# A two-layer cross-attention kernel on one core: last tile's end in two halves, weight loads on another queue, and a new written order

## What is computed

```
# layer 0
q = LN(x) @ Wq ; k, v = LN(ctx) @ Wkv                    # 16 heads
x = x + softmax(q k^T * hd**-0.5) v @ Wproj + bproj
x = x + gelu(LN(x) @ W1 + b1) @ W2 + b2                   # hidden 1024
# layer 1
q = unit(rotate(rms(x) @ wq)) ; k = unit(rotate(ctx @ wkv[k])) ; v = ctx @ wkv[v]
x = x + softmax(q k^T * hd**0.5) v @ wout
```

## Time and profile before

| what | us |
|---|---|
| median of 3 runs | 341.33 |
| lowest and highest | 341.09, 341.97 |
| the profiled execution's own time | 343.29 |
| span of its core, first to last instruction | 341.5 |
| TensorE busy (PE) in that span | 330.3 |
| VectorE, ScalarE, GpSimd busy | 266.7, 230.6, 193.2 |

### The profile page before, as it was taken

The page is one execution under the profiler, slowest core; times in us unless marked ns, Lnnn a source line. Parts: engine busy times, 40 slices in busy tenths (PEclk is TensorE's granted clock), DMA queues, the critical chain, the costliest instruction groups (busy, mean ns, idle before and its releaser), DMA issues.

```text
span 341.5 us, 10106 instructions
## 1 busy us (share of the span) xinstructions
PE 330.3 (97%) x3929; PEld 295.5 (87%) x3929; DVE 266.7 (78%) x586; ACT 230.6 (68%) x422; POOL 193.2 (57%) x200
## 2 busy tenths in 40 slices
PE   7899999999999999999999999999998999999995
PEld 7877876888778887899999999999998998888884
DVE  2969989988998669778788788666579989887643
ACT  3568876787775653885736665655678867789871
POOL 3585675886542202635857987493662799647100
PEclk9899999999999999999999999999999999999998
DMA  5667411110020000100000010000000000010101
GB/s 155 200 207 234 138 33 31 33 34 2 3 94 2 3 3 2 33 3 0 3 31 2 0 33 3 31 2 32 2 2 0 3 2 33 17 36 33 50 33 63
DMA packets 13007, 13.79 MB, mean 40 GB/s; under 512 B 1440, under 2 KB 12192, under 8 KB 12960
## 3 DMA queue, kind: packets, MB, share of 16 engines
q1 hardware_dynamic: 12240, 12.34, 11.4%
q10 hardware_dynamic: 720, 0.80, 0.8%
HBM read 11.04 MB, written 2.10 MB: 38 GB/s over the span
## 4 chain that ended last, share of the span: by engine, by line
PE 81%; DVE 6%; issue 4%; POOL 3%; ACT 2%; DMA 1%; ACTq 1%; POOLq 0%; DVEq 0%
PE banks_s L1326 12%; PE bank_y L1121 5%; PE banks_s L1216 5%; PE banks_s L1234 4%; PE banks_s L1393 4%; PE bank_o L1121 4%; PE bank_t L1337 4%; PE bank_y L1337 3%; PE bank_t L1121 3%; PE bank_o L1135 2%; PE bank_y L1135 2%; PE bank_o L1266 2%; PE bank_qk L1337 2%; PE bank_o L1337 2%; DVE row_max L2233 2%
## 5 line engine op out<-in xcount | busy, mean ns | idle before, releaser
L436 POOL TENSOR_TENSOR norm_q_inv<-norm_q_min,minus_half 128x32 f32<-128x32 f32 x8 | 43.8, 5476 | 21.0 <-DVE norm_q_min L2416 19.4
L424 POOL TENSOR_TENSOR norm_k_inv<-norm_k_min,minus_half 128x32 f32<-128x32 f32 x8 | 44.5, 5566 | 12.8 <-DVE norm_k_min L2383 12.7
L659 ACT ACTIVATE PT<-banks_s 128x1024 f32<-128x1024 f32 x32 | 31.0, 1023 | 15.7 <-PE banks_s L1243 15.7
L2233 DVE TENSOR_REDUCE row_max<-banks_s 128x8 f32<-128x1024 f32 x32 | 37.6, 1218 | 4.3 <-PE banks_s L1216 4.0
L703 ACT ACTIVATE W_s<-banks_s,small_t 128x256 f32<-128x256 f32 x60 | 25.2, 471 | 20.1 <-PE banks_s L1326 20.0
L1326 PE MATMUL banks_s<-lnT_hi,W_hi 128*128 128x256 f32 x120 | 34.4, 287 | 0.0
L1326 PE MATMUL banks_s<-lnT_hi,W_lo 128*128 128x256 f32 x120 | 33.9, 283 | 0.0
L1326 PE MATMUL banks_s<-lnT_lo,W_hi 128*128 128x256 f32 x120 | 33.9, 283 | 0.0
L685 ACT ACTIVATE PT<-banks_s 128x1024 f32<-128x1024 f32 x32 | 31.2, 1024 | 3.6 <-PE banks_s L1393 3.6
L712 ACT ACTIVATE hT_hi<-W_s 128x512 fp32r<-128x512 f32 x32 | 20.0, 632 | 15.8 <-PE bank_y L1337 10.1
L389 POOL TENSOR_TENSOR x_all<-x_all,b_row 128x256 f32<-128x256 f32 x16 | 12.4, 794 | 27.2 <-DVE b_xn L2316 25.4
(11 more groups left out here) (375 smaller groups left out, 1088.6 us busy)
## 6 DMA issues: line engine op xcount, KB each, us to landing
x_all<-in_x SPq DMA_DIRECT2D x16, 128.0 KB, 2.2
ctx_in<-in_ctx_wide SPq DMA_DIRECT2D x16, 128.0 KB, 2.5
W_s<-in_L_xattn_W SPq DMA_DIRECT2D x2, 1024.0 KB, 7.8
ctx_in<-in_ctx_T SPq DMA_DIRECT2D x8, 256.0 KB, 2.6
out<-x_all SPq DMA_DIRECT2D x16, 128.0 KB, 1.7
W_s<-in_L_xattn_Wq ACTq DMA_DIRECT2D x1, 256.0 KB, 3.4
W_s<-in_L_xattn_Wkv ACTq DMA_DIRECT2D x1, 256.0 KB, 4.5
W_s<-in_L_xattn_Wkv ACTq DMA_DIRECT2D x2, 128.0 KB, 4.8
```

The lines of the kernel that those rows point to most:

```text
L424: nc.gpsimd.tensor_tensor(norm_k_inv[:, :], norm_k_min[:, :], minus_half[:, :], ALU.pow).then_inc(c_kinv, 1)
L436: nc.gpsimd.tensor_tensor(norm_q_inv[:, :], norm_q_min[:, :], minus_half[:, :], ALU.pow).then_inc(c_qinv, 1)
L659: nc.scalar.activation(PT[:, t % 2, 2 * h:2 * h + 2, :], banks_s[:, 2 * h:2 * h + 2, :], ACT.Exp, scale=HD ** -0.5).then_inc(a_exped, 1)
L2233: v.tensor_reduce(row_max[:, 8 * h:8 * h + 8], banks_s[:, 2 * h:2 * h + 2, :].rearrange("p n (r k) -> p (n r) k", k=TOK), AX.X, ALU.max).t ...
```

## The change

1. **Wkv on the other queue.** The three loads of Wkv leave ScalarE's queue and stand on SyncE's, behind the loads of tiles 0 and 1 and ahead of the wait for them.
2. **Tile 31's end in two halves of eight heads.** weighted_first(31) and weighted_second(31) go to different banks, and out_T, back, heads_out, normed, out_hi, out_lo and project of tile 31 become two calls each. The number of transposes and matmuls is the same; ScalarE gets two instructions more, VectorE three more.
3. **A new order on all four engines**, with new banks and new free-standing waits to match. Steps, operands and counts are otherwise the same, but for idle(7), which becomes idle(8).

The diff, cut to its core:

```diff
             load_x(1)
             load_ctx(1)
+            sp.dma_start(Wkv_s[:, 0, :], Wkv[0:128, :]).then_inc(wkv_loaded, LOADED)
+            for half in (slice(0, C2B), slice(C2B, 128)):
+                sp.dma_start(Wkv_s[half, 1, :], Wkv[128:C2, :]).then_inc(wkv_loaded, LOADED)
             sp.wait_ge(wkv_loaded, 3 * LOADED)
...
             act.dma_start(Wq_s, Wq.rearrange("(t p) n -> p t n", p=128)).then_inc(wq_loaded, LOADED)
-            act.dma_start(Wkv_s[:, 0, :], Wkv[0:128, :]).then_inc(wkv_loaded, LOADED)
-            for half in (slice(0, C2B), slice(C2B, 128)):
-                act.dma_start(Wkv_s[half, 1, :], Wkv[128:C2, :]).then_inc(wkv_loaded, LOADED)
...
+            def out_T_half(h, bank):
+                act.wait_ge(av, 4 * NB - 1 + h)
+                act.wait_ge(o_back, 2 * NB - 1)
+                nc.scalar.activation(oT[:, in_pair(h, 2 * TOK)], bank[:, in_pair(h, 2 * TOK)], ACT.Copy).then_inc(oT_ready, 1)
+            def out_hi_half(h, bank):
+                act.wait_ge(on_transposed, 2 * NB + h)
+                act.wait_ge(proj_mm, 2 * NB - 1)
+                nc.scalar.activation(onT_r[:, 0, h, :], bank[:, in_pair(h, TOK)], ACT.Copy).then_inc(onT_hi, 1)
...
+            def back_half(h, bank):
+                pe.wait_ge(oT_ready, 2 * NB + h)
+                for g in (2 * h, 2 * h + 1):
+                    last = nc.tensor.transpose(bank[:, 128 * g:128 * g + 128], oT[:, 128 * g:128 * g + 128], ident[:, :])
+                last.then_inc(o_back, 1)
+            def project_half(h, bank):
+                pe.wait_ge(onT_lo, 2 * NB + h)
+                for n, (x, y) in enumerate(HI_LO):
+                    last = mm(bank[:, 0:C1], onT_r[:, x, h, :], wout_r[:, y, h, :], start=h == n == 0, stop=h == 1 and n == 2)
...
# TensorE's list, the start
             query_bias(0, bank_o)
             kv_bias(0, bank_y)
-            rows_T(0, bank_t)
-            context_T(0, bank_qk)
-            idle(7)
             pe.wait_ge(a_bq, 1)
+            rows_T(0, bank_o)
+            context_T(0, bank_t)
+            idle(8)
...
# TensorE's list, the end
-            weighted_first(31, bank_o)
-            weighted_second(31, bank_o)
+            weighted_first(31, bank_y)
+            weighted_second(31, bank_qk)
             pe.wait_ge(onT_lo, 30)
-            project(29, bank_y)
+            project(29, bank_o)
+            pe.wait_ge(oT_ready, 32)
+            back_half(0, bank_y)
             pe.wait_ge(on_ready, 31)
             normed(30, bank_t)
-            pe.wait_ge(oT_ready, 32)
-            back(31, bank_o)
+            pe.wait_ge(oT_ready, 33)
+            back_half(1, bank_qk)
             pe.wait_ge(res_ready, 30)
+            normed_half(0, bank_o)
+            pe.wait_ge(on_ready, 32)
             project(30, bank_y)
-            pe.wait_ge(on_ready, 32)
-            normed(31, bank_o)
+            pe.wait_ge(onT_lo, 31)
+            normed_half(1, bank_t)
             pe.wait_ge(onT_lo, 32)
-            project(31, bank_o)
+            project_half(0, bank_o)
+            project_half(1, bank_o)
# VectorE's list, the end
             heads_out(30, bank_t)
-            residual(29, bank_y)
+            residual(29, bank_o)
+            heads_half(0, bank_y)
             out_lo(30, bank_t)
-            heads_out(31, bank_o)
+            heads_half(1, bank_qk)
             residual(30, bank_y)
-            out_lo(31, bank_o)
+            out_lo_half(0, bank_o)
+            out_lo_half(1, bank_t)
             residual(31, bank_o)
```

1623 lines of the change are left out of this document (822 added, 801 removed).

## The result

The changed kernel takes 344.37 us (median of 4 runs, 344.11 to 344.73) against 341.33 us before. The ratio is 1.0087, with a 95% interval of 1.0069 to 1.0104: 3.0 us slower. I had forecast 339.9, with a range up to 343.4. Only four runs of before stand behind the 341.33; in the later comparisons its median lies between 341.84 and 342.11, and against those the changed kernel is 2.3 to 2.5 us slower.

The account below looks back on a forecast made before the run. TensorE, busy 97% of the span, was taken as the bound, with stage 1's score-bank loop nearly as tight. Terms -0.9, -0.2, +0.6 and -0.9 gave -1.4 us: 339.9 from the median 341.33, range 336.8 to 343.4.

Parts of the forecast that it names:

- The start, -0.9: Up to scores_a(0): earlier normalising and splitting bring scores_a(0) to 19.15 from 20.11; -0.9 us, bounds -1.9 and +0.6.
- The end, -0.2: Tile 31's halves: last residual near 338.75 instead of 338.94, project(30) delayed; -0.2 us, bounds -0.9 and +0.2.
- Stage 1, +0.6: scores_a(1) to scores_a(15): counting +0.6, waits mended -1.0, new waits +1.0; sum +0.6 us, bounds -4 and +3.
- The counting of gaps: Stage 1: TensorE's calls summed against each gap's room; new list over by 9.6 us against 9.0, so +0.6.
- back(3)'s wait: Stage 1: 0.8 us wait for its copy, mended by values_mm_a(3) standing between; about 1.0 with another wait.
- the 0.45 at back(8): Stage 1, after scores_a(10): a new 0.45 us wait, with ScalarE's out_T(8) behind four calls.
- Stages 2 and 3, -0.9: Order in stages 2 and 3: two TensorE waits go, small losses added; -0.9 us, bounds -1.3 and +2.
- The wait at inputs_c(4): Stages 2 and 3: TensorE's 0.9 us wait for a bank should go, since the call uses another bank.
- the one at 197.6: Stages 2 and 3: 0.4 us wait for GpSimd's context split should go, context calls being earlier on TensorE.
- The slower one: Stage 1, maxima(3) to maxima(9): VectorE becomes the bound, 93% busy with 2.0 us more work; 343.0 us, chance 0.22.
- No-change: Whole kernel: the start gives nothing and the lists otherwise balance; 341.3 us, chance 0.18.

Follow-up runs that it names:

- middle_ctx: Kernel before with the new start and halved end, and GpSimd's context_hi(0) and context_lo(0) moved behind masked_second(13): 340.93 us, 0.9961 of before.
- middle_both: middle_ctx plus weighted_second(3) behind scores_a(5), out_T(3) ahead of rows_hi(4), and clamp_c(1) behind context_lo(3): 340.60 us, 0.9962 of before.
- mix_stage1_before: Changed kernel with before's lists at the start and in stage 1, the changed lists behind: 343.34 us, 1.0040 of before.
- mix_start_before: Changed kernel with before's lists and Wkv loads up to the calls around scores_a(3): 345.02 us, 1.0085 of before.

## Why the prediction was wrong, step by step

The four terms of -0.9, -0.2, +0.6 and -0.9 came to about 0, -0.2, +1.7 and +1.6 against a run of before at full clock. Three steps failed: the reference of the start, VectorE's calls taken at their undisturbed length in stage 1, and the waits in stages 2 and 3 that were followed on TensorE's list but not on GpSimd's.

- **The start, -0.9.** Against the profile the direction was right and the size too small (rows_T(0) 10.39, scores_a(0) 18.50; forecast 10.8 and 19.15). Wkv was there at 7.5, not 8.0, and the clock stayed at 1.00. The step that failed is the reference: I subtracted from a profiled execution that had the stretch at half clock and stood 2.0 us above the median. Against a run without that stretch no gain is shown (18.25 to 19.30 with the new start, 18.67 and 19.22 with before's). I had written the half of it down (343.29 against 341.33) and then let 341.5 stand for the median.
- **The end, -0.2.** Right: 39.48 to 39.31, with project(30) 0.2 later and the last residual 0.17 earlier from scores_c(8) on, as followed (36.93 to 36.76). The same residual comes at 36.69 in middle_ctx and middle_both, though their spans end 39.58 and 39.48 behind scores_c(8): what follows the last residual varies by 0.3 us between profiles.
- **Stage 1, +0.6.** From scores_a(1) to scores_a(15) it became 1.3 us longer than in the earlier trace rows, and 2.0 longer than in an undisturbed run (106.9). The counting of gaps took every VectorE call at its length without GpSimd beside it; the contention cost 1.5 us. Of the waits that I saw, maxima(10) is 0.33 us late for 0.5 and back(3)'s wait is gone; the 0.45 at back(8) didn't come (no wait over 0.34 us before scores_a(11)), and scores_turned(9) starts 0.6 us behind its maxima instead of 1. Those at maxima(5) and (6), 1.7 us, I didn't see: they need GpSimd's list beside VectorE's. The +0.6 of the counting itself may have been right: 0.7 us of the loss are left once the contention is gone.
- **Stages 2 and 3, -0.9.** Measured +1.55. The wait at inputs_c(4) went, and one as long came at values_mm(7), one call ahead of scores_c(0); the one at 197.6 went and a larger one, 0.75 us, came at 169.8, whose mend gave 0.7. I reasoned that the context calls were earlier on TensorE's list and so safe; they were earlier, and GpSimd's half of them wasn't. The further 0.69 at back(21) is a bank that queries_c(7) still holds; its mend failed, so its price is not shown.
- **The rivals.** The slower one had the place, the sign and most of the size (VectorE at 95%, late maxima, and 2.2 us between scores_a(5) and scores_a(8)). VectorE had 5.1 us more busy time there, where the rival counted 2.0. Its mechanism, two calls more in six periods, was not the cause: with GpSimd moved away the same calls fit. No-change was right on the start alone. The range ended at 343.4, since stages 2 and 3 had +2 as a bound of their own but the rival's 343.0 was built on their forecast gain: no case held both losses.

## What to carry to other kernels

Before costing a change against a profile, set the profiled run beside the median, and find the rows that make the difference; a gain that only removes what the median doesn't have is no gain. When work is reordered across engines, lay GpSimd's list beside VectorE's and let a VectorE instruction that reads two SBUF tensors end its own width (1.1 ns a column here) behind the GpSimd instruction that runs beside it; and look ahead of each single long instruction on any queue for the short one behind it that others wait for. A wait is worth its length only if nothing else ends just behind it: of seven attempts on a wait of TensorE, one gave its full length, one 0.34 of 1.06 us, and five left it, moved it or made it longer.

## What the runs showed of the hardware

- A 128x128 subtraction on VectorE took 344 to 350 ns alone and 846 and 1353 ns beside GpSimd's subtractions; a 128x16 one 0.18 and 0.72 us; a 128x512 one 0.69 and 1.11 us. They ended 0.03 us (16 columns), 0.15 (128), 0.28 (256) and 0.55 (512) after GpSimd's instruction. Instructions that read a bank didn't change (0.68 and 1.21 us).
- TensorE's granted clock is at or near its lower level (0.50, which is 1.2 GHz, and 0.62 over the same 3.4 us) in both profiles of before, after a wait of TensorE of 1.27 and 1.26 us ahead of rows_T(0), and at 1.00 in mix_stage1_before and mix_start_before after waits of 1.08 and 0.71. In the changed kernel the wait is 0.28. Runs with the lower mean clock have 1.0 us more of span.
- Apart from such meetings the lists run alike to a few hundredths: kernels that share a list agreed on its stretches of 23 to 90 us mostly within 0.05 us, on three chips. Away from the start and from such meetings one profile prices a moved call, where the timed comparison leaves 0.5 us open.
